# Norm's transposes behind the output projection, folded weights in quarters, roots ahead of the last context, the first gate product ahead of the routing transposes

## What is computed

```python
x = x + tanh(g_xattn) * xattn(layernorm(x), ctx)      # 16 heads of 64; 128 context rows of 64
x = x + tanh(g_ffn) * ffn(layernorm(x))
# xattn: softmax((q Wq)(kv Wk)^T / 8) (kv Wv), all heads, then Wo and bo
# ffn: a sigmoid router picks 8 of 32 experts (2 of 4 groups first);
#      out = sum_e w_e * (silu(x Wg_e) * (x Wu_e)) Wd_e + a shared expert of the same form
```

## Time and profile before

| | |
|---|---|
| median of 3 runs | 639.36 us (638.5 to 640.11) |
| the profiled execution | 639.41 us, its span 637.6 us |
| busy share of the span | PE 98%, PEld 77%, DVE 84%, ACT 63%, POOL 51% |
| TensorE's granted clock | 9 of 10 or more in all 40 slices |
| before chunk 0 | 0 to 20.5 us |
| chunk 0 | 20.5 to 57 us |
| chunks 1 to 6 | 57 to 292 us, 39 us each |
| chunk 7 | 292 to 328 us |
| experts | 328 us to the end, 38 us a chunk |

### The profile page before, as it was taken

One profiled execution on the slowest core, in us unless ns is written; L12 is line 12 of the kernel. 1 busy time (PEld: TensorE's weight loads), 2 busy tenths in 40 slices (PEclk: granted clock), 3 DMA queues, 4 the chain that ended last, 5 costly groups with the idle time before them and its releaser, 6 DMA issues.

```text
span 637.6 us, 13965 instructions
## 1 busy us (share of the span) xinstructions
PE 626.7 (98%) x3761; PEld 488.5 (77%) x3761; DVE 534.1 (84%) x1376; ACT 400.0 (63%) x742; POOL 328.2 (51%) x376
## 2 busy tenths in 40 slices
PE   8999999999999999999999999999999999999998
PEld 6657787777777787777678788787887878788786
DVE  6999989899998999989879879697786958869565
ACT  5665676777767776776655465555555555565554
POOL 5226543545545445544207556565665656656654
PEclk9999999999999999999999999999999999999999
DMA  6233233232332333322238274542637445274650
GB/s 176 89 101 88 78 89 90 69 82 67 98 82 67 85 86 75 84 84 75 71 82 214 69 166 116 133 121 73 162 84 163 121 92 132 69 177 103 144 141 17
DMA packets 58429, 65.60 MB, mean 103 GB/s; under 512 B 26256, under 2 KB 35344, under 8 KB 58384
## 3 DMA queue, kind: packets, MB, share of 16 engines
q1 hardware_dynamic: 58384, 65.07, 40.2%
HBM read 61.64 MB, written 2.88 MB: 101 GB/s over the span
## 4 chain that ended last, share of the span: by engine, by line
PE 84%; DVE 6%; issue 3%; DMA 3%; SPq 1%; POOL 1%; DVEq 1%; ACT 0%; POOLq 0%
PE bank L1344 17%; PE bank L1345 17%; PE bank L1346 17%; PE bank L1466 8%; PE bank L1442 6%; PE bank L1391 4%; PE bank L1433 2%; PE bank L1431 2%; PE bank L1430 2%; PE bank L1411 2%; PE bank L1420 1%; PE bank L1414 1%; PE bank L1417 1%; PE bank L1351 1%; DMA inverse_bc<-inverse_dram 1%
## 5 line engine op out<-in xcount | busy, mean ns | idle before, releaser
L614 POOL TENSOR_TENSOR halves<-area,halves 128x512 fp32r<-128x512 f32 x134 | 174.3, 1301 | 138.1 <-ACT halves L768 133.0
L789 ACT ACTIVATE area<-bank 128x512 f32<-128x512 f32 x136 | 81.4, 599 | 108.8 <-PE bank L1346 105.7
L1300 DVE TENSOR_TENSOR bank<-area,bank 128x512 f32<-128x512 f32 x128 | 88.6, 692 | 49.9 <-PE bank L1346 49.6
L1344 PE MATMUL bank<-x2t_hi,w_hi 128*128 128x512 f32 x272 | 110.2, 405 | 0.1
L1345 PE MATMUL bank<-x2t_hi,w_lo 128*128 128x512 f32 x272 | 107.2, 394 | 0.0
L1346 PE MATMUL bank<-x2t_lo,w_hi 128*128 128x512 f32 x272 | 106.2, 391 | 0.0
L542 POOL TENSOR_TENSOR ctx_hi<-ctx_raw,ones_col 128x128 fp32r<-128x128 f32 x32 | 27.7, 866 | 137.8 <-DMA ctx_raw<-ctx_t 137.2
L768 ACT ACTIVATE halves<-area 128x512 fp32r<-128x512 f32 x136 | 85.1, 626 | 19.5 <-DVE area L1311 18.4
L898 DVE TENSOR_REDUCE row_max<-bank 128x4 f32<-128x512 f32 x128 | 82.0, 683 | 12.4 <-PE bank L1391 11.4
L712 ACT ACTIVATE area<-bank 128x512 f32<-128x512 f32 x128 | 68.3, 593 | 33.5 <-PE bank L1420 33.5
L1311 DVE TENSOR_TENSOR area<-bank,wbc 128x512 f32<-128x512 f32 x128 | 86.4, 680 | 0.7 <-DMA wbc<-rows_dram 0.6
(11 more groups left out here) (170 smaller groups left out, 1253.8 us busy)
## 6 DMA issues: line engine op xcount, KB each, us to landing
wbc<-rows_dram SPq DMA_DIRECT2D x126, 256.0 KB, 4.3
inverse_bc<-inverse_dram SPq DMA_DIRECT2D x64, 256.0 KB, 3.5
w_raw<-experts SPq DMA_DIRECT2D x32, 102.0 KB, 2.5
x_sb<-x SPq DMA_DIRECT2D x8, 256.0 KB, 3.3
ctx_raw<-ctx_t SPq DMA_DIRECT2D x32, 64.0 KB, 2.9
ctx_keys<-ctx_nat SPq DMA_DIRECT2D x32, 64.0 KB, 2.3
out<-area SPq DMA_DIRECT2D x7, 256.0 KB, 4.0
max_rows<-max_t SPq DMA_DIRECT2D x64, 4.0 KB
```

The costliest lines, as they stand in the source:

```text
L614: nc.gpsimd.tensor_tensor(hid_lo[:, u % SLOTS, :], hid[:, u % HIDS, :], raw(hid_hi[:, u % SLOTS, :]), ALU.subtract).then_inc(hidlo_ready, 1)
L789: nc.scalar.activation(silu_g[:, u % 2, :], gate_ps[u % 2][:], ACT.Silu).then_inc(silu_ready, 1)
L1300: nc.vector.tensor_tensor(up_ps[u % UPS][:], silu_g[:, u % 2, :], up_ps[u % UPS][:], ALU.mult)\
L1344: nc.tensor.matmul(ps, wh, xh, start=start, stop=False)
```

## The change

The four edits are in the order of instructions and in the size of some; the arithmetic is the same. (1) In chunks 1 to 6 `transpose_norm` stands behind `project_out`. (2) `inverse_root` stands ahead of the last `split_context` of chunk 0. (3) The first folds go into four banks, and `a_high` and `a_low` work in four quarters of 256 columns instead of two halves of 512; DVE makes all quarters ahead of its second `apply`; the second transposes of chunk 0's tokens come behind three banks of `g_project(0)`, and the transpose of batch 0's maxima behind three banks of `g_project(1)`; ACT and DVE follow this order. (4) The first gate product stands ahead of `transpose_weights(0)`.

```diff
--- before.py
+++ after.py
@@ -183,7 +183,7 @@
         st_ps = (bank[2:4], bank[4:6])
         u_ps = st_ps
         g_ps = (bank[0], bank[1], bank[6], bank[2])
-        fold_ps = (bank[0], bank[2])
+        fold_ps = bank[0:4]
         xt_ps = bank[6:8]
         early_ps = ((bank[6:8], bank[4:6]), (bank[0:2], bank[4:6]))
         gate_ps, up_ps, route_ps, y_ps, misc_ps = bank[0:2], bank[2:5], bank[5], bank[6], bank[7]
@@ -598,10 +598,10 @@
                     add_bias(t, c)
                     if last and b == 2:
                         x2t_low(0, 0)
+                    if first and b == CB - 1:
+                        inverse_root(0, 2, slice(2 * CB, NB))
                     if not last:
                         split_context(b, t + CB, c + 1)
-                if first:
-                    inverse_root(0, 2, slice(2 * CB, NB))
 
             pool.wait_ge(bo_ready, 1)
             in_chunks(pool, attention)
@@ -675,11 +675,11 @@
                 nc.scalar.activation(silu_low, ps[:, CB * NE:2 * CB * NE], ACT.Silu if c > 0 else ACT.Exp)\
                     .then_inc(sig_ready, 1)
 
-            def a_high(i):
-
-                act.wait_ge(fold_done, i + 1)
-                half = slice(4 * i, 4 * i + 4)
-                nc.scalar.activation(a_hi[:, half, :], fold_ps[i][:].rearrange("p (h n) -> p h n", h=4), ACT.Copy,
+            def a_high(j):
+
+                act.wait_ge(fold_done, j // 2 + 1)
+                nc.scalar.activation(a_hi[:, 2 * j:2 * j + 2, :],
+                                     fold_ps[j][:, 0:2 * P].rearrange("p (h n) -> p h n", h=2), ACT.Copy,
                                      scale=SCALE).then_inc(ahi_ready, 1)
 
             act.wait_ge(early_step, 1)
@@ -687,7 +687,8 @@
             nc.scalar.activation(tanh_g[:], early_v[:, 0:2], ACT.Tanh)
             a_high(0)
             xt_high_half(0)
-            a_high(1)
+            for j in range(1, 4):
+                a_high(j)
             g_high(0, 0, range(2), bank)
             xt_high_half(1)
             g_high(0, 0, range(2, 4), bank)
@@ -695,9 +696,9 @@
             nc.scalar.activation(tanh_g[:], gates[:], ACT.Tanh).then_inc(tanh_ready, 1)
             act.wait_ge(tanh_ready, 1)
             nc.scalar.activation(bo_gated[:], bo_bc[:], ACT.Copy, scale=tanh_g[:, 0:1]).then_inc(bo_ready, 1)
-            g_high(1, 1, range(3), bank)
+            g_high(1, 1, range(2), bank)
             max_out(0, 0, 0)
-            g_high(1, 1, range(3, 4), bank)
+            g_high(1, 1, range(2, 4), bank)
             for i in range(2):
                 act.wait_ge(fold_done, i + 3)
                 nc.scalar.activation(c_pair[:, 4 * i:4 * i + 4, :],
@@ -1104,20 +1105,22 @@
                 .then_inc(rstd_step[0], RSTD_STEPS)
             dve.wait_ge(rstd_step[0], RSTD_STEPS)
             apply(0, 0, range(2))
-            def a_low(i):
-
-                dve.wait_ge(ahi_ready, i + 1)
-                half = slice(4 * i, 4 * i + 4)
-                nc.vector.scalar_tensor_tensor(a_lo[:, half, :], fold_ps[i][:].rearrange("p (h n) -> p h n", h=4), SCALE,
-                                               raw(a_hi[:, half, :]), ALU.mult, ALU.subtract).then_inc(alo_ready, 1)
+            def a_low(j):
+
+                dve.wait_ge(ahi_ready, j + 1)
+                nc.vector.scalar_tensor_tensor(a_lo[:, 2 * j:2 * j + 2, :],
+                                               fold_ps[j][:, 0:2 * P].rearrange("p (h n) -> p h n", h=2), SCALE,
+                                               raw(a_hi[:, 2 * j:2 * j + 2, :]), ALU.mult, ALU.subtract)\
+                    .then_inc(alo_ready, 1)
 
             a_low(0)
             xt_low_half(0)
+            for j in range(1, 4):
+                a_low(j)
             apply(0, 0, range(2, 4))
-            a_low(1)
-            g_low(0, 0, range(2), bank)
+            g_low(0, 0, range(1), bank)
             xt_low_half(1)
-            g_low(0, 0, range(2, 4), bank)
+            g_low(0, 0, range(1, 4), bank)
             for h in range(2):
                 for q in range(2):
                     take_max(0, 0, h, q, early_ps[0][h])
@@ -1368,8 +1371,7 @@
                     if bank_free is not None:
                         s, value = bank_free[j // 2]
                         wait(pe, s, value + j % 2)
-                    if j % 2 == 0:
-                        pe.wait_ge(alo_ready, j // 2 + 1)
+                    pe.wait_ge(alo_ready, j + 1)
                     for i in range(2):
                         p = 2 * j + i
                         cols = slice(ring * 2 * P, (ring + 1) * 2 * P)
@@ -1467,10 +1469,12 @@
                 ins.then_inc(attn_done, 1)
 
 
-            def fold(left, right, i, ps):
+            def fold(left, right, i, banks):
                 for j in range(4):
                     p = 4 * i + j
-                    ins = nc.tensor.matmul(ps[:, j * P:(j + 1) * P], left[:, p, :], right[:, p, :], start=True, stop=True)
+                    each = 4 // len(banks)
+                    ins = nc.tensor.matmul(banks[j // each][:, j % each * P:(j % each + 1) * P], left[:, p, :],
+                                           right[:, p, :], start=True, stop=True)
                 ins.then_inc(fold_done, 1)
 
             def keep_busy(products, weights, ps):
@@ -1481,23 +1485,24 @@
             pe.wait_ge(warm_ready, 1)
             keep_busy(WARM_UP, c_pair, small_ps)
             pe.wait_ge(wqk_in[0], 16 * 3)
-            fold(wq_pair, wk_diag, 0, fold_ps[0])
+            fold(wq_pair, wk_diag, 0, fold_ps[0:2])
             pe.wait_ge(const_ready, 6)
             transpose_half(0)
             pe.wait_ge(wqk_in[1], 16 * 3)
-            fold(wq_pair, wk_diag, 1, fold_ps[1])
-            g_project(0, 0, None, range(2))
+            fold(wq_pair, wk_diag, 1, fold_ps[2:4])
+            g_project(0, 0, None, range(3))
             transpose_half(1)
-            g_project(0, 0, None, range(2, 4))
+            g_project(0, 0, None, range(3, 4))
             pe.wait_ge(xlo_ready, 1)
             max_scores(0, 0, 0, 0, early_ps[0][0])
             max_scores(0, 0, 0, 1, early_ps[0][1])
-            g_project(1, 0, ((glo_ready, 1), (glo_ready, 3)))
+            g_project(1, 0, ((glo_ready, 1), (glo_ready, 3)), range(3))
             transpose_max(0, 0)
+            g_project(1, 0, ((glo_ready, 1), (glo_ready, 3)), range(3, 4))
             pe.wait_ge(wvo_in, 16 * 3)
-            fold(wv_diag, wo_pair, 0, early_ps[0][0][0])
+            fold(wv_diag, wo_pair, 0, early_ps[0][0][0:1])
             pe.wait_ge(maxt_ready, 1)
-            fold(wv_diag, wo_pair, 1, early_ps[0][0][1])
+            fold(wv_diag, wo_pair, 1, early_ps[0][0][1:2])
             pe.wait_ge(glo_ready, 4 + 2)
             max_scores(1, 1, 0, 0, early_ps[1][0])
             max_scores(1, 1, 0, 1, early_ps[1][1])
@@ -1521,7 +1526,7 @@
                         scores(t, b, nth, 1, nth + 1, None)
                         if not (last and b >= 2):
                             max_scores(t + 2, b + 2, nth + 1, 1)
-                    if b == 1:
+                    if b == 1 and (first or last):
                         transpose_norm(c + 1, ut_ps)
                     if last and b == CB - 1:
                         pe.wait_ge(max_ready, 4 * NB)
@@ -1529,6 +1534,8 @@
                         pe.wait_ge(x2_ready, t - 3)
                     if not (first and b < 3):
                         project_out(t - 3, (b + 1) % 2, t + 1 if last and b == CB - 1 else t + 2)
+                    if b == 1 and not first and not last:
+                        transpose_norm(c + 1, ut_ps)
                     for q in range(2):
                         if first or last:
                             weigh(t, b, 0, q, c + 1)
@@ -1548,8 +1555,6 @@
             pe.wait_ge(u_ready, 4 * NB - 2)
             pe.wait_ge(x2_ready, NB - 3)
             project_out(NB - 3, (NB - 3) % 2, NB)
-            transpose_weights(0, y_ps)
-
 
             def weight_halves(kind, u):
                 cols = slice(kind * FW + u * P, kind * FW + (u + 1) * P)
@@ -1588,6 +1593,8 @@
                         pe.wait_ge(x2lo_ready, c + 1)
                     wait(pe, silu_ready, free_of(2, c, u))
                     split_product(gate_ps[u % 2][:], weight_halves(0, u), x2_halves[parity]).then_inc(gate_done, 1)
+                    if first and u == 0:
+                        transpose_weights(0, y_ps)
                     if first and u == 2:
                         pe.wait_ge(u_ready, 4 * NB)
                     wait(pe, hid_ready, free_of(UPS, c, u))
```

## The result

The changed kernel takes 641.99 us (median of 8 runs, 640.98 to 643.21) against 638.96 for the kernel before, measured beside it (8 runs, 638.5 to 640.11). The ratio is 1.0044 with a 95% interval of 1.0035 to 1.0054: about 3 us slower, where 2.4 us faster was forecast. The sign is wrong, and the time lies outside the range.

What follows compares the result with a forecast made beforehand. TensorE, busy 98% of the span, was taken as the bound, so gains come only from its stops. Terms -2.3, -0.6, +0.35 and +0.1 summed to -2.45, giving 637.0 us, range 636.0 to 638.4.

Steps and rivals of the forecast that it cites:

- Its first half: Chunks 1 to 6: with transposes behind the projection, the 0.54 stop for `xn` goes, 2.8 us in all.
- The chain behind them: Transposes, `xnt_hi` copy on ACT, `xnt_lo` on DVE: 1.94, or 2.09 with three hand-overs, against 2.00 of PE work.
- DVE's 2.3 us of waiting at `row_max`: DVE's wait for PE in each chunk, claimed to cover its lateness behind `xnt_lo`, ten times what is needed.
- The condition I set myself: Prediction wrong if the new wait ahead of `g_project` is above 0.3, or `row_max` begins before 14.
- the 0.54 of idle time: PE's stop ahead of the transposes in a steady chunk, claimed as gained in full with nothing added or dropped.
- The forecast loss of 0.5 at `g_project`: PE stops 0.09 ahead of `g_project` for `xnt_lo` in each of six chunks, 0.5 in all.
- the two collisions and the lateness: Moved roots on POOL collide with two DVE normalisations, not one; end later by up to one's length, still ahead of DVE.
- the bound to take: Roots moved ahead: bounds -0.5 and -0.8; -0.6 taken with POOL still splitting weights, -0.8 were POOL clear of `probs_low`.
- late by 0.4: Start of chunk 0: folds and second `max_scores` 0.4 late, the following `row_max` waits; +0.35 taken for all that follows.
- The place of the stop: Moved gate product: PE stops about 0.5 in sum at the up products of units 5 and 6.
- The slower one: Late `xnt_lo` lets `g_low` hold up `scores` every chunk; needs above 0.8 a chunk, at 1.0 time 642.4; chance 0.05.
- the third rival: `xnt_hi` and `xnt_lo` each wait for a copy, 0.3 a chunk; transposes' move gives -1.0, time 638.3; chance 0.25.

Runs made afterwards that it cites:

- The best order: Kernel before, with the transposes behind the projection's fourth pair of eight in chunks 1 to 6 and the residual ahead of `xnt_lo`: 637.19 us, ratio 0.9972.
- the second kernel: Kernel before with quarters and second transposes behind three weight products, but the maxima transposed after all four second weight products: 639.72 us, ratio 1.001.
- the third kernel: Kernel before with quarters alone, PE's order and the order of the `g_low` copies as before: 639.2 us, ratio 1.0003.

## Why the prediction was wrong, point by point

The four edits alone measured +1.9, -0.7, +1.75 and +0.1 us by the medians. Their sum, 3.05, fits the loss of the change, 3.0, so nothing asks for a term that only shows when the edits stand together; by the four intervals the sum is uncertain by about 1.3 (an estimate).

**Edit 1: -2.3 forecast, +1.6 to +1.9 measured.** Its first half held: the stop for `xn` went, and the transposes stood 2.37 behind `max_scores`, forecast 2.32. The chain behind them held as well: from their start to the end of `xnt_lo` it took 112.12 - 110.08 = 2.04, forecast 1.94 and two hand-overs. The step that failed is "DVE stands idle for 0.2 in front of `xnt_lo` and everything queued behind it is that much later: residual, reciprocal, two normalisations", with its conclusion that DVE's 2.3 us of waiting at `row_max` cover this lateness. The lateness itself was nearly right (0.30 for the residual, counted from `max_scores`); the cover was the wrong one. I named the residual and did not ask who waits for it. PE does, in `transpose_max`, half a microsecond later and ahead of `g_project`. DVE did catch up as forecast (its own waits at `row_max` in a chunk fell from 2.3 to 1.7), but what was late had been asked for long before that. The experiment with the residual first shows the cause: it changes the order of two DVE instructions and the wait goes. The condition I set myself, a new wait above 0.3, came true at another instruction than `g_project`. A second step was mis-sized: the 0.54 of idle time was priced in full, less 0.09. The best order got back 0.28 of it, since `g_project` is then held by `xnt_lo`: its load follows the end of `xnt_lo` by 0.22, where before 0.68 lay between the two.

**The forecast loss of 0.5 at `g_project`** was 0.09 a chunk. Where nothing else stands in front, it is 0.20, 1.2 in all: right mechanism, half of the size.

**Edit 2: -0.6 forecast, -0.7 measured.** The roots began at 53.29 (forecast 53.24) and ended at 59.14, a microsecond later than the 58.0 of the text, since two of the twelve steps took 1.23 and 1.28 us instead of 0.23, where before only one was long (1.12, at 57.16). In those two stretches DVE ran normalisations, at 53.28 for 1.15 and at 56.85 for 1.22. This agrees with what the Trainium skill (SBUF — State Buffer, Who interferes with whom) says of a VectorE instruction with two inputs in SBUF beside a GpSimd one that reads SBUF, and with the two collisions and the lateness that the prediction worked out from it. DVE did not wait. `probs_low` took 0.90 in the changed kernel, with POOL at work beside it (`w_hi`, L563, from 61.39 for 0.53), so -0.6 was the bound to take; -0.6 and -0.8 cannot be told apart by the time.

**Edit 3: +0.35 forecast, +1.75 measured (1.1 to 2.4 by its interval).** The mechanisms are those of the text: `row_max` 14.32 in the second kernel, with the fold at 6.73 (forecast 14.2), the stop of 0.68 in front of the transpose of the maxima (0.8), the first product at 9.13 (9.07). What was mis-sized is its end, "late by 0.4": the whole edit has 0.83 in its trace (0.95 in the run without edit 1, where the first folds together took 1.50 in place of 1.05). The difference from 0.83 to 1.75 is not found at the start of the program. The lateness is still 0.88 at the transpose of batch 28's maxima, then 1.37 at the routing transposes and 1.79 at the end. But the second and the third kernel lose as much between batch 28 and the end (0.98 and 0.95), and the third ends level with before all the same. So part of it may be a quick end of the one execution of before that the profile shows. What makes the difference stays open; the last attention chunk alone varies by as much, as the last section tells.

**Edit 4: +0.1 forecast, +0.1 measured** (-0.6 to +0.8 by its interval, so that the size is not shown). That the load is late with the store fits the added wait for `wbc`, 0.8 in two against 0.6 in one. The place of the stop was wrong: not the up products but a projection.

**The rivals.** The slower one had 0.05 and the condition that the lateness "is not caught up by the next batch". Its 642.4 lies next to the measured 641.99, but by luck. It was the right engine and the right instruction, but its condition and its price of 0.8 a chunk were not what happened: 0.26 a chunk with the gain already lost is what edit 1 costs, and edit 3 gives almost as much again. In its form ("the stop moves instead of going"), the third rival came nearest, with -1.0 for the edit instead of +1.9, because it looked for the stop at the copies only.

## What to carry to other kernels

When a move makes one instruction late, list for every instruction queued behind it on its engine who waits for it and when, not only whether that engine catches up by its next long wait. Here the costly one was a 0.28 us residual, awaited as a guard for a bank. Its place in PE's program can be asked about as well: the transpose writes columns 0 to 127 of that bank and the projection columns 128 to 255, and what the guard also keeps is the next batch's projection, which has no wait of its own for the residual. Whether it could stand there, no run tried. Where a wait is too early in one place and its result too late in the next, try a place between, and let the short result that others wait for go first: together with the roots this gave 2.2 us, where the written change lost 3. And an idle time in the list need not be what can be had: of 0.54 a chunk the best order got 0.28.

## What the runs showed of the hardware that was not expected

**What stands between two matmuls costs time when PE has no lead, even where nothing is late.** From the load of `transpose_max`'s weights to that of `g_project` it took 0.34 in the changed kernel (112.39 and 112.73), 0.31 with edit 1 alone and 0.31 with the transposes in the middle, in all of which PE had just been held up at `transpose_max` and `xnt_lo` had ended 0.6 ahead of the load. The two matmuls start 0.35 apart in the first of them; where PE came from six long matmuls without a stop, as before, they start 0.03 apart. Where `xnt_lo` came last, its end was followed by the load after 0.21 with the residual first (111.68 to 111.89), 0.22 with both moves and 0.20 with the roots as well. From the end of the residual to `transpose_max`'s load it was 0.07 (112.32 to 112.39). In the program as it is built two register additions, the first without a wait and the second with that for `xnt_lo`, an instruction with the wait for `a_lo` and the first product's own wait for its bank stand between the first pair; behind the wait for the residual stands only `transpose_max`'s own wait. So the time grows with the instructions that are left, some 0.1 each (an estimate from these distances). Whether the waits or the register additions make it is not shown: no run took one of them out.

**One execution is not like the next at the start and in the last attention chunk.** The first fold, which waits for its weights to be loaded, began between 5.66 and 6.73 us. The last attention chunk, from the transpose of the maxima of batch 29 to the routing transposes, took 40.8 before, 41.0 in the changed kernel, 42.2 with edit 1 alone and 41.9 with the residual first, though of these only the changed kernel alters it, by one gate product. Each is one execution, so that what varies there was not found. A difference below 1 us between two traces says nothing there; the medians of a dozen runs say more.
